# One step of the shared expert handed from GpSimd to VectorE, two weight splits moved, and the first two routed tiles prepared inside the shared expert

## The reference

```python
x2 = rmsnorm(hid, ln2_w).reshape(-1, h)
...
top_w, top_i = jax.lax.top_k(probs, TOPK)
...
gu = jnp.einsum('th,eih->tei', x2, w1)
g, u = (gu[..., :I], gu[..., I:])
act = jax.nn.silu(g) * u
down = jnp.einsum('tei,ehi->teh', act, w2)
routed = jnp.einsum('te,teh->th', wfull, down)
sgu = x2 @ sh_gu_w.T
sg, su = (sgu[..., :SHI], sgu[..., SHI:])
shared = jax.nn.silu(sg) * su @ sh_down_w.T
return hid + (routed + shared).reshape(b, s, h)
```

## Time and profile before

| | |
|---|---|
| time, median of 3 runs | 1249.02 us (1248.98 to 1249.04) |
| time of the profiled execution | 1255.6 us |
| its span in the trace | 1253.8 us |
| TensorE busy | 1180.2 us, 94% |
| VectorE busy | 861.2 us, 69% |
| ScalarE busy | 795.3 us, 63% |
| GpSimd busy | 576.2 us, 46% |
| shared expert, first product to last | 954.6 to 1027.4 us |
| first product of the routed experts | 1030.6 us |

### The profile page before, as it was taken

How to read it: one execution, slowest core, us unless ns; L and a number is a source line. 1 busy time by engine, 2 the same in 40 slices (tenths; PEclk the granted TensorE clock), 3 DMA queues, 4 the chain that set the end, 5 groups by cost and what they waited for, 6 DMA issues and landing times.

```text
span 1253.8 us, 25173 instructions
## 1 busy us (share of the span) xinstructions
PE 1180.2 (94%) x7996; PEld 1010.8 (81%) x7996; DVE 861.2 (69%) x2662; ACT 795.3 (63%) x1971; POOL 576.2 (46%) x845
## 2 busy tenths in 40 slices
PE   6899999799999999999999999999988869999986
PEld 5756555589999998999999999989987759999962
DVE  5677887567667666886777877678855845555535
ACT  3487787667778776677777777776776524444432
POOL 3053654544333444537343365434353426666650
PEclk9989999899999999999999999999999989999998
DMA  8955555165632112122212122111214246777767
GB/s 270 284 158 173 177 161 161 46 189 154 197 122 94 54 52 89 52 69 80 82 35 68 35 98 73 40 63 34 70 59 115 69 119 105 117 119 117 118 99 238
DMA packets 111780, 139.59 MB, mean 111 GB/s; under 512 B 11364, under 2 KB 94820, under 8 KB 111524
## 3 DMA queue, kind: packets, MB, share of 16 engines
q1 hardware_dynamic: 97204, 119.10, 31.3%
q0 software_dynamic: 14448, 18.88, 9.4%
HBM read 63.36 MB, written 61.87 MB: 100 GB/s over the span
## 4 chain that ended last, share of the span: by engine, by line
PE 72%; DVE 11%; ACT 8%; issue 4%; POOL 2%; DMA 1%; another core or an unknown queue 1%; SPq 0%; POOLq 0%; ACTq 0%; DVEq 0%
PE bank L1461 52%; PE bank L1669 5%; PE bank L1851 5%; PE bank L1510 3%; DVE bank L1102 3%; PE bank L1547 2%; PE bank L1530 2%; ACT pT L827 2%; ACT p L942 1%; DVE hs L1319 1%; PE bank L1537 1%; PE bank L1830 1%; PE bank L1861 1%; POOL sum_rows L737 1%; DVE pT L1306 1%
## 5 line engine op out<-in xcount | busy, mean ns | idle before, releaser
L1102 DVE CUSTOM_DVE_ANT_0 bank<-bank,mask 128x512 f32<-128x512 f32 (+3 forms) x512 | 235.4, 524 | 38.0 <-PE bank L1530 22.4
L933 ACT ACTIVATE p<-bank,stat 128x512 f32<-128x512 f32 (+3 forms) x256 | 131.7, 528 | 132.1 <-DVE stat L1102 132.0
L528 POOL CAST w_hl<-raw_qkv 128x512 fp32r<-128x512 f32 x96 | 58.9, 614 | 313.1 <-DMA raw_qkv<-in_qkvo 161.0
L1461 PE MATMUL bank<-xT,w_hl 128*128 128x512 f32 x768 | 189.3, 395 | 3.0 <-DVE hs L1319 3.0
L1461 PEld LDWEIGHTS bank<-xT,w_hl 128*128 128x128 f32 x768 | 144.1, 188 | 37.4 <-issue 3.5
L737 POOL DMA_INDIRECT sum_rows<-mid,goal x79 | 122.9, 1556 | 78.2 <-DVE mid L1425 75.5
L1461 PE MATMUL bank<-pT,v 128*128 128x128 f32 (+3 forms) x768 | 137.5, 328 | 0.0
L1461 PE MATMUL bank<-qk 128*128 128x512 f32 (+3 forms) x768 | 130.9, 319 | 2.9 <-DVE pT L1306 2.6
L942 ACT ACTIVATE p<-p,stat 128x512 f32<-128x512 f32 (+3 forms) x256 | 123.1, 553 | 14.7 <-DVE stat L1322 14.5
L1461 PEld LDWEIGHTS bank<-qk 128*128 128x128 f32 x768 | 120.4, 191 | 11.9 <-DVE v L1300 2.8
L529 POOL TENSOR_TENSOR w_hl<-raw_qkv,w_hl 128x512 fp32r<-128x512 f32 x96 | 124.3, 1295 | 7.8
(11 more groups left out here) (232 smaller groups left out, 2405.9 us busy)
## 6 DMA issues: line engine op xcount, KB each, us to landing
raw_qkv<-in_qkvo SPq DMA_DIRECT2D x32, 768.0 KB
xs_rows<-blank SPq DMA_DIRECT2D x32, 520.0 KB, 3.5
xs_rows<-blank SPq DMA_DIRECT2D x5, 2730.0 KB, 14.3
xrow<-xs_rows SPq DMA_DIRECT2D x79, 130.0 KB, 2.5
raw_o<-in_qkvo SPq DMA_DIRECT2D x32, 256.0 KB
sum_rows<-blank SPq DMA_DIRECT2D x3, 2176.0 KB, 8.4
stk<-xT SPq DMA_DIRECT2D x96, 64.0 KB
stk<-k_hl SPq DMA_DIRECT2D x96, 64.0 KB
```

Of the source, the lines that this page charges most:

```text
L933: act.activation(p2[:, n % 2, POFF[qi]:POFF[qi + 1]], s2(t), ACT.Exp, scale=-1.0, bias=stat2[:, 0, n % 2, t:t + 1], accum_out=stat2[:, 1, ...
L1102: return dve.tensor_tensor_reduce(scores, scores, mask[:, TB - scores.shape[1]:], scale=-1.0, scalar=-2.0 * MASKED, op0=ALU.add, op1=ALU.m ...
L1461: ins = pe.matmul(out, a, b, start=start and i == 0, stop=stop and i == len(pairs) - 1, **kw)
```

## The change

Four edits are made together.

- Step 0's low part is taken from GpSimd's list and put into VectorE's, ahead of `norm_half2`. The waits are counted anew.
- The two late weight splits of VectorE (`w1_rest(1, 0)` and `w1_rest(1, 1)`) stand behind steps 8 and 10, no longer behind steps 10 and 11.
- `xtt` gets memory of its own, and ScalarE's wait for the last `shared_down` falls away.
- The first two tiles are turned by TensorE between `shared_down(10)` and `shared_down(11)` (all that is left of `shared_up` is done by then), and VectorE splits them ahead of the last batch's add of the shared expert's result into `hs`.

```diff
+            xtt = sb(l3, "xtt", [P, 2, 2, D], F32R)
...
-        xtt = sh_hi[:, :, :].rearrange("p r n -> p (r n)")[:, 0:4 * D].rearrange("p (i a n) -> p i a n", i=2, a=2)
...
+        W1_LATE = (SHARED - 4, SHARED - 2)
...
-            for s in range(LO_POOL):
+            for s in range(1, LO_POOL):
                 shared_lo(s)
...
                 if i >= 2:
                     act.wait_ge(e_up, i - 1)
-                else:
-                    act.wait_ge(f_dn, SHARED)
...
+                if s == SHARED:
+                    take_x(0)
+                    take_x(1)
                 if s and s % SHR == 0:
...
-                if LO_POOL <= s < SHARED:
+                if s == 0 or LO_POOL <= s < SHARED:
                     dve.wait_ge(f_hh, s + 1)
...
-                if s >= SHARED - 2 and s < SHARED:
-                    w1_rest(1, s - SHARED + 2)
...
-            take_x(0)
-            take_x(1)
+                if s in W1_LATE:
+                    w1_rest(1, W1_LATE.index(s))
...
-                if s < LO_POOL:
-                    pe.wait_ge(f_lop, s + 1)
+                if 1 <= s < LO_POOL:
+                    pe.wait_ge(f_lop, s)
                 else:
-                    pe.wait_ge(f_lod, s - LO_POOL + 1)
+                    pe.wait_ge(f_lod, s - LO_POOL + 2 if s else 1)
...
+                if s == SHARED:
+                    for i in range(2):
+                        pe.wait_ge(f_h, SHARED - 1 + i)
+                        turn_tile(i)
                 if s:
                     shared_down(s - 1)
...
-            pe.wait_ge(r_tabi, 1)
-            expert = [pe.value_load(tab[0:1, P:P + 1], min_val=0, max_val=E - 1)]
...
-            turn_tile(0)
-            turn_tile(1)
+            pe.wait_ge(r_tabi, 1)
+            expert = [pe.value_load(tab[0:1, P:P + 1], min_val=0, max_val=E - 1)]
             pe.wait_ge(w_lo, 2 * C)
```

More of the change, by code:

```diff
@@ L1360, in w1_rest, with take_x @@
                                          ALU.mult, ALU.subtract).then_inc(w_lo, 1)
+            def take_x(i):
+                dve.wait_ge(e_xh, i + 1)
+                dve.tensor_tensor(xtt[:, i % 2, LO, :], bank[2 + i % 2][:, 0:D], f32(xtt[:, i % 2, HI, :]),
+                                  ALU.subtract).then_inc(e_xl, 1)
             for s in range(SHARED + 1):
@@ L1402, in _ @@
                     dve.tensor_copy(tab[0:1, :], bank[4][0:1, 0:2 * P]).then_inc(r_tabi, 1)
-                if s >= SHARED - 2 and s < SHARED:
-                    w1_rest(1, s - SHARED + 2)
-            def take_x(i):
-                dve.wait_ge(e_xh, i + 1)
-                dve.tensor_tensor(xtt[:, i % 2, LO, :], bank[2 + i % 2][:, 0:D], f32(xtt[:, i % 2, HI, :]),
-                                  ALU.subtract).then_inc(e_xl, 1)
-            take_x(0)
-            take_x(1)
+                if s in W1_LATE:
+                    w1_rest(1, W1_LATE.index(s))
             for i in range(NT + 2):
@@ L1797, in shared_down, with turn_tile @@
                 ins.then_inc(f_dn, 1)
+            def turn_tile(i):
+                pe.wait_ge(e_x[i % NX], 16 * (i // NX + 1))
+                if i >= 2:
+                    pe.wait_ge(e_xl, i - 1)
+                for c in range(C):
+                    ins = pe.transpose(bank[2 + i % 2][:, P * c:P * (c + 1)], xt[:, i % NX, P * c:P * (c + 1)], ident[:, :])
+                ins.then_inc(e_t, 1)
             pe.wait_ge(s_ok, SHR)
@@ L1820, in _ @@
                     ins.then_inc(r_tabT, 1)
-            pe.wait_ge(r_tabi, 1)
-            expert = [pe.value_load(tab[0:1, P:P + 1], min_val=0, max_val=E - 1)]
-            def turn_tile(i):
-                pe.wait_ge(e_x[i % NX], 16 * (i // NX + 1))
-                if i >= 2:
-                    pe.wait_ge(e_xl, i - 1)
-                for c in range(C):
-                    ins = pe.transpose(bank[2 + i % 2][:, P * c:P * (c + 1)], xt[:, i % NX, P * c:P * (c + 1)], ident[:, :])
-                ins.then_inc(e_t, 1)
             def up(i):
```

## The result

The changed kernel takes 1254.09 us, the median of 5 runs (1252.24 to 1256.05); the kernel before, run beside it, took 1249.02 (5 runs, 1246.48 to 1249.49). The ratio is 1.0041 with an interval of 1.0029 to 1.0054: **slower by 5.1 us**, where 5.8 us of gain was forecast, and outside the range. The profiled execution took 1252.24 us with a span of 1250.4.

What follows compares the result with a forecast made beforehand. It took TensorE's idle places to bound the kernel, with the stalls of steps 9 and 10 ending with GpSimd's last send. 3.15 + 1.8 + 0.9 = 5.85 us off 1249.02 gave 1243.2 us, range 1241.8 to 1249.4.

Steps and rivals of the forecast that it cites:

- What bounds the kernel: TensorE busy 94% of the span; its waits at the stretch's beginning and end, and stalls tied to the sends, matter.
- The idle time of steps 9 and 10: VectorE's 4.95 and ScalarE's 5.05 us waits during GpSimd's sends, no engine named; taken to end with the last send.
- The end, 3.15 us: At the shared expert's end, `up(0)` starts at 1027.41 instead of 1030.56, behind no VectorE work: 3.15 us gained.
- the tiles' loads end last: Rival, 23%: first tiles' loads bind, `up(0)` comes 1.5 to 2.5 us later; gain -0.4 to 0.6 us.
- The clock, 1.8 us: From `up(0)` to the fourth tile's `up`, full clock without the idle time ahead: 1.8 us gained, bounds 0 and 1.8.
- The low part of step 0, 0.9 us: At the beginning, `shared_down(0)` starts 1.1 us sooner, logits and sends 0.6 to 1.2 sooner; 0.9 taken.
- The split moved to step 8: VectorE's 3.14 us split at about 1005 is covered by its 4.22 us of idle time: no cost.
- the split delays the sends: Rival, 8%: VectorE's split shuts out GpSimd's descriptor writes, sends up to 3.14 us late; 2.7 us gain, 1246.3.
- The queues: In SyncE's loads, the fifth tile lands with 0.7 us to spare: nothing counted, up to 1 us for the bound.
- The range: Forecast's own range 1242 to 1245.5 us; whole range 1241.8 to 1249.4, up to the loads rival's upper end.
- the first stretch: The part from step 0's low part to the logits' reduction, claimed to come 0.6 to 1.2 us sooner.
- Slower: Rival, 7%: same lock with the loads last; sends and loads 2.2 us later, `shared_down(11)` 1 us more; 1252.2 us.

Runs made afterwards that it cites:

- e0: The kernel before, unchanged, run again for a second profile: 1247.49 us, ratio 0.9997.
- e3: The kernel before with only the first two tiles' edits (own memory for `xtt`, turned and split early): ratio 1.0008.
- e4: The changed kernel with the two late weight splits put back behind steps 10 and 11: ratio 1.0006.
- e1: The kernel before with only the two late weight splits moved, behind steps 8 and 10: ratio 1.0019.
- g1: The kernel before, with VectorE's early split waiting for GpSimd's low part of step 2 and eight tile loads ahead of the second-layer weights: 1245.35 us, ratio 0.9965.
- g2: g1 with each late weight split cut into four pieces of 128x704 at the same places: 1245.16 us, ratio 0.9964.
- h1: The kernel before, with only VectorE's wait for GpSimd's low part of step 2 ahead of the early split: ratio 0.9986.
- e2: The kernel before with only step 0's low part moved from GpSimd to VectorE: ratio 0.9995.
- e5: The changed kernel with the second input of the two late weight splits read from PSUM, which alters some low parts: ratio 0.9982.
- e7: The changed kernel with the first eight tile loads, not four, ahead of the last second-layer weights: ratio 1.0002.

## Why the prediction was wrong, point by point

**What bounds the kernel.** This is the step that failed: "I take it that the sends hold this up, and that the resume goes with the last send." The idle time of steps 9 and 10 was taken for the kernel's own and put at the base of every term, though the rows named no releaser and the execution was 6.6 us longer than the median. Without it the last shared product ends 2.9 us before the first tile is there (e0), and the loads end last, behind sends that VectorE's splits hold up. What that idle time was in the one profile stays open.

**The end, 3.15 us.** Nothing. It priced a wait that the kernel hardly ever has. The rival "the tiles' loads end last" described the true case: `shared_down(11)` stands behind the second load, and `up(0)` comes 2.3 us later against the load, inside the 1.5 to 2.5 it gave. By the second sum 0.6 to 0.8 of it is left (e3, e4 and the changed kernel against before). Two things give the rest back. In e0 most of the first two tiles' work runs at half clock, and from `up(0)` to the third tile's `up` it takes 4.81 us; in the changed kernel the twelve products have taken a part of the slow time, and it takes 3.80. And before lost 0.81 us at the fifth tile (0.36 for its load, 0.45 behind it), the changed kernel 0.42.

**The clock, 1.8 us.** Nothing, for the same reason. TensorE idled 7.24 us and `up(0)` ran at 0.50. The prediction's point that the clock "falls" after 2.21 us and not after 1.74 was a rule from two cases: behind the same 2.2 us it fell in five of the nine profiles named under e1 (0.54 and 0.61 in e0's windows behind it), and stayed at 1.00 in four (g1 is one), with the same instructions up to there.

**The low part of step 0, 0.9 us.** The steps up to the logits were right, and the size is 1.2 us, the upper end, against an execution in which the clock fell. All of it is the clock's: where the clock stayed up, before has its logits at 12.14 us too, with the idle time of 2.2 still there, and the edit brings nothing. And behind the logits the sign turned. With the logits 1.25 us sooner, `w1_rest(0, 1)` starts 12.9 us after step 0's `gated`, not 14.2. GpSimd's low part of step 2 starts at 13.0 in both (13.3 at the latest, in g2 and h1). So the split now wins the race by 0.1 us, the low part takes 4.16 us, `shared_down(2)` idles 2.56, and the first send comes 2.0 later. In before the order goes either way, with the clock, as said under e1; with the edit and no wait GpSimd's low part lost it in all five profiles (changed, e2, e4, e5, e7). The lock that the prediction discussed for the sends and for the root was never tried on this pair. For the root it came true: one step of it took 0.63 us instead of 0.20 beside VectorE's new subtraction, and ScalarE's work hid that.

**The split moved to step 8, nothing.** It cost 2.05 us: two held sends (4.06 and 2.74 us) for one (3.72). The idle time that was to cover it was the one that isn't there. The rival "the split delays the sends" was weighed down by the subtraction beside a send (1.05 against 0.97). But that row is for the rival, if one asks when the send ended: 994.62 plus 1.05 is 995.67, and that is 0.86 us after the subtraction's end (994.13 plus 0.68), the same distance as behind a split of 3.14. The send met only the last 0.19 us of a short instruction, so it lost little; a send inside a split of 3.14 meets much more of it. By the Trainium skill, page "SBUF — State Buffer", section "SBUF: two separate sides", a VectorE instruction with two SBUF inputs and a GpSimd instruction that reads SBUF shut each other out for their whole length; by that rule, the trace agrees: 3.1 us on a send, 2.9 on the low part of step 2, none with one input in PSUM. The rule stood on the page, and a row that bears it out was read as one against it.

**The queues.** "I count nothing, and up to 1 us for the bound": the fifth tile's load behind twelve weight transfers was worth 0.9 us in e7, at the bound.

**The range.** The forecast's own lower end, 1242, lies 0.9 us under what its terms give: with all 1.2 of the first stretch it is 1242.9. That did no harm here; the time came out at the other side.

**The rivals.** "Slower" (7%) named the lock with the loads last, and gave 1252.2. It had two of the three mechanisms, and without the race at step 2 it falls short by 1.9 us. That its 2.2 us for the sends is near the measured 2.05 is luck: it took 0.9 off for sooner sends, which came later, and didn't know that a send of before is held as well. Its two conditions were held unlikely each by itself, but they were one: with the idle time gone, the loads end last and the splits lie beside the sends. They should have had one chance together, and a large one.

## What to carry to other kernels

Where the profiled execution is longer than the plain runs by more than the change may bring, and it holds an idle time without a releaser about that long, price the change without it first. Where VectorE's instructions with two inputs in SBUF are moved, list what GpSimd does beside each old and new place, its scattered transfers included, compare the ends of the two and not only their lengths, and look at who starts first: an engine that comes 1.25 us sooner can lose 2 us by overtaking the other. An order that the clock decides is worth a wait that fixes it.

## What the runs showed of the hardware

- A scattered send of GpSimd's, 0.97 us alone, took 2.7 to 4.1 us beside a VectorE multiply-subtract of 128x2816 with both inputs in SBUF, and ended 0.84 us after it. Beside a VectorE subtraction of 0.68 us it took 1.02 to 1.44 and ended 0.84 to 0.87 us after it. With one input of the split from PSUM it took 1.00.
- GpSimd's subtraction of 96x512 took 4.16 us for 1.28 when it began 0.11 us after such an instruction. When GpSimd's began first, VectorE's was held: a comparison of 128x24 took 1.31 us for 0.18 beside a subtraction of GpSimd's of 1.37.
- Four pieces of 128x704 back to back, 3.53 us, held one send for 4.46 us; others, begun beside a single piece, ended 0.85 us after that piece and took 1.4.
- After an idle time of TensorE of 2.2 us, with the same instructions ahead of it, the granted clock fell in five profiles and stayed at 1.00 in four; behind an idle time of 1.07 us, in the changed kernel, it stayed at 1.00.
